# One group of attention scores is issued ahead of the transposes of the next x in TensorE's loop

## What is computed

```
xn = layernorm(x)
q, k = l2norm(xn Wq), l2norm(xn Wk);  v = xn Wv        # 16 heads of 16
p = softmax(q k^T + bias)                              # bias: only 0 <= key - query < 128, minus a slope times the distance
s = (p v) Wo
g = silu(fp4_linear(silu(fp4_linear(xn, w_gate)) * fp4_linear(xn, w_up), w_down))
out = x + s * g
```

## Time and profile before

| | |
|---|---|
| median of 3 runs | 502.65 us (501.77 to 503.2) |
| the profiled execution | 503.14 us, of it a span of 501.4 us in the trace |
| PE busy | 451.2 us, 90% of the span |
| DVE, ACT, POOL busy | 441.2, 402.5, 409.6 us |
| DMA engines, mean over the span | 59 GB/s |

### The profile page before, as it was taken

How to read it: one execution, slowest core, us unless ns; L and a number is a source line. 1 busy time by engine, 2 the same in 40 slices (tenths; PEclk the granted TensorE clock), 3 DMA queues, 4 the chain that set the end, 5 groups by cost and what they waited for, 6 DMA issues and landing times.

```text
span 501.4 us, 14045 instructions
## 1 busy us (share of the span) xinstructions
PE 451.2 (90%) x4990; PEld 314.2 (63%) x4990; DVE 441.2 (88%) x897; ACT 402.5 (80%) x584; POOL 409.6 (82%) x897
## 2 busy tenths in 40 slices
PE   0378889999999999999999999999999999999997
PEld 0144556666667666676767676667666766666665
DVE  4989989999989999989989999988998999887686
ACT  1466988988888888888887888888888888888952
POOL 6544678899988888889997898989999888887751
PEclk9857999999999999999999999999999999999999
DMA  8211011224321314223221222222422121222100
GB/s 300 88 43 44 6 37 44 65 75 76 75 63 45 45 41 67 64 64 64 66 65 43 64 34 54 65 54 54 54 54 54 44 24 43 54 54 54 44 22 33
DMA packets 78276, 29.35 MB, mean 59 GB/s; under 512 B 67712, under 2 KB 77696, under 8 KB 78208
## 3 DMA queue, kind: packets, MB, share of 16 engines
q1 hardware_dynamic: 77920, 28.39, 24.7%
q10 hardware_dynamic: 288, 0.08, 0.1%
HBM read 7.49 MB, written 4.19 MB: 23 GB/s over the span
## 4 chain that ended last, share of the span: by engine, by line
PE 53%; ACT 20%; issue 11%; DVE 10%; POOL 3%; DMA 1%; ACTq 0%; DVEq 0%; POOLq 0%
PE gt L351 10%; PE up L351 10%; PE gt L551 9%; ACT probs L1341 8%; PE bank_q L351 8%; PE bank_b L357 5%; ACT L1341 4%; PE gt L573 4%; ACT pv_t L1219 3%; ACT qk_sq L1319 3%; PE bank_b L598 2%; PE scores L505 2%; PE gt L555 1%; DMA qk_slots<-qk_stack 1%; PE gt L357 1%
## 5 line engine op out<-in xcount | busy, mean ns | idle before, releaser
L1341 ACT ACTIVATE probs<-scores 128x1024 f32<-128x1024 f32 (+1 forms) x101 | 102.2, 1012 | 2.3 <-PE scores L505 1.2
L1526 POOL TENSOR_SCALAR_AFFINE_SELECT probs<-probs 128x512 f32<-128x512 f32 x128 | 81.9, 641 | 1.7 <-ACT probs L1341 1.3
L1533 POOL TENSOR_SCALAR_AFFINE_SELECT probs<-probs 128x512 f32<-128x512 f32 x120 | 76.2, 637 | 3.7
L598 PE MATMUL bank_b<-probs,vals 128*32 128x128 f32 x1952 | 59.7, 274 | 0.6 <-DVE vals L944 0.3
L598 PEld LDWEIGHTS bank_b<-probs,vals 128*32 128x32 f32 x1952 | 51.6, 110 | 7.4 <-issue 5.7
L1219 ACT ACTIVATE qk_stack<-bank_q 128x512 f16<-128x512 f32 x64 | 35.1, 595 | 22.3 <-DVE bank_q L923 22.3
L793 DVE SCALAR_TENSOR_TENSOR xT_lo<-gt,xT_hi 128x512 f16<-128x512 f32 (+1 forms) x34 | 22.3, 657 | 26.3 <-ACT xT_hi L1219 26.3
L551 PE MATMUL gt<-wdn_hi,hT_hi 128*128 128x256 f16 x160 | 43.6, 273 | 0.6 <-DVE hT_lo L845 0.6
L551 PE MATMUL gt<-wdn_hi,hT_lo 128*128 128x256 f16 x160 | 43.6, 273 | 0.0
L551 PE MATMUL gt<-wdn_lo,hT_hi 128*128 128x256 f16 x160 | 43.6, 273 | 0.0
L1563 POOL TENSOR_TENSOR h_q<-h_grid,h_scale 128x704 f32<-128x704 bf16 x31 | 43.1, 1391 | 0.0
(11 more groups left out here) (219 smaller groups left out, 1468.5 us busy)
## 6 DMA issues: line engine op xcount, KB each, us to landing
out<-y SPq DMA_DIRECT2D x32, 128.0 KB, 1.9
x_all<-x SPq DMA_DIRECT2D x20, 128.0 KB, 2.0
x_all<-x SPq DMA_DIRECT2D x3, 512.0 KB, 4.1
x_all<-wproj SPq DMA_DIRECT2D x1, 768.0 KB, 6.9
dn_raw<-wd SPq DMA_DIRECT2D x1, 704.0 KB, 8.7
probs<-wg SPq DMA_DIRECT2D x1, 640.0 KB, 5.3
probs<-wu SPq DMA_DIRECT2D x1, 640.0 KB, 7.6
qk_slots<-qk_stack SPq DMA_TRANSPOSE x32, 3.7
```

The lines of the kernel that those rows point to most:

```text
L598: done = e.matmul(pv_bank(i)[32 * n:32 * n + 32, grp * P:(grp + 1) * P], va, pr, start=part == 0, stop=part == 1 or final(i))
L1341: e.activation(probs[j % P_BUFS][:, grp, :, side(j), :], score_banks(j, grp)[:, :, :, side(j), :].rearrange("p b e h q -> p (b e) h q"), A ...
L1526: e.affine_select(out=own, in_=own, compare_op=ALU.is_ge, fill=0.0, base=0, pattern=[[0, GRP], [-1, P]], channel_multiplier=1).then_inc(s_ ...
L1533: e.affine_select(out=part, in_=part, compare_op=ALU.is_gt, fill=0.0, base=0, pattern=[[0, GRP], [1, P]], channel_multiplier=-1).then_inc( ...
```

## The change

Two lines of TensorE's loop change places. No instruction is added or removed, and every wait stays with its instruction.

```
@@ -666,8 +666,8 @@
             gate_mm_last(2)
             v_mm(4)
             for t in range(4, 31):
+                scores(t - 1, 0)
                 tr_x(t + 1)
-                scores(t - 1, 0)
                 scores(t - 1, 1)
                 pv(t - 3)
                 scores(t - 1, 2)
```

## The result

| | before | changed |
|---|---|---|
| median of 22 runs | 502.18 us | 503.88 us |
| lowest to highest | 501.63 to 503.3 | 502.76 to 505.12 |
| profiled execution, its span | 503.14, 501.4 us | 502.76, 501.0 us |

The account below looks back on a forecast made before the run. A turn was taken as 5.10 us of ScalarE from silu to keep_pv, then about 8.95 us of TensorE. Terms 0 + 0 + 0 + 1.3 us on the 502.65 us median gave 503.9 us; range about 501.9 to 505.8 us.

Parts of the forecast that it names:

- First and second step: TensorE's loop: scores 0 moves into the wait for silu, tr_x unchanged, then scores 1 and pv 0.22 us earlier.
- Third step: Ahead of tr_tail: the 0.22 us only lengthen TensorE's idle time, 0.69 for 0.47 us, behind ScalarE's stretch; 0 us.
- Fourth step: Scores 0's moved wait for the DMA transpose: landings over 1.08 us after silu's start cost the excess; three turns, 1.3 us.
- Rival B: Late transposes weigh more: five to seven turns at 0.5 us, +2.5 to +3.5 us, 505.2 to 506.2 us; chance 0.33.
- the bound of no change: The forecast itself: no change that can be told, between -0.3% and +0.3% (1.5 us); chance 0.59.
- Rival C: TensorE, not ScalarE, holds tr_tail, so 0.22 us is gained each turn: 5.9 us less, 496.7 us; chance 0.08.

Follow-up runs that it names:

- e4: Kernel before (old order) with the four products of scores group 1 repeated three more times, same values, in tiles 3 to 29: 511.13 us, ratio 1.0178.
- e5: Changed kernel (new order) with the four products of scores group 1 repeated three more times, same values: 509.56 us, ratio 1.0152 against the kernel before.
- e1: Kernel before with the two lines swapped only in the 20 loop turns whose DMA transposes had been regular there: ratio 1.0013.
- e2: Kernel before with the two lines swapped only in the seven loop turns whose DMA transposes had been slow there: ratio 1.0021.
- e11: Changed kernel with 64 small float16 products (128 instructions, half a code block) at the head of TensorE's program: 505.13 us, ratio 1.0053 against the kernel before.
- e12: Kernel before (old order) with 64 small float16 products (128 instructions) at the head of TensorE's program: 502.51 us, ratio 0.9999.
- e10: Changed kernel with 64 small float32 products (256 instructions, a whole code block) at the head of TensorE's program: 523.34 us.
- e3: Changed kernel with scores group 0 issued one step further ahead, in front of v_mm of the turn before: 504.67 us, ratio 1.0043 against the kernel before.

## Why the prediction was right, and where it wasn't

First and second step (scores 0 into silu's wait; tr_x no later; pv 0.22 us earlier): as forecast, to 0.01 us, in the timeline after. Turn 17, where a sequence begins, gained 0.03 us (13.36 to 13.33), within the 0.1 us that it was given. With 13.36 us there and 13.81 us in the loop's first turn, the 14.05 us hold for 25 of the 27 turns.

Third step (the gain is hidden by ScalarE, 0 us): right, shown by regular turns of 14.05 us, by idle time of 0.69 us ahead of tr_tail, and by e4 and e5, where taking the cover away makes the 0.22 us appear.

Fourth step (landing minus s+1.08): the mechanism is shown by e1, e2, e11 and e12, and the point was 0.03 us too early: from landing to tr_tail it takes 3.99 us (359.68 to 363.67), not 4.02, since pv to tr_tail takes 2.73 us and not the 2.76 that were read from the loop's first turn. Ten late swapped turns with their excess, from four kernels:

| L | 1.16 | 1.19 | 1.34 | 1.37 | 1.43 | 1.45 | 1.54 | 1.66 | 1.77 | 1.98 |
|---|---|---|---|---|---|---|---|---|---|---|
| excess, us | 0.05 | 0.09 | 0.23 | 0.27 | 0.33 | 0.35 | 0.43 | 0.56 | 0.67 | 0.87 |

Each is L - 1.11 within 0.02 us, and so are four more in e10. Only turn 17, where a sequence begins and the exponentials are half as long, has less slack: in e11 it lost 0.58 us at L = 1.29. The old order's point, by the one turn that passed it (22 of e12), is 1.80, 0.69 us later.

The sum of 1.3 us came out as 1.4 us over the runs, but its three terms didn't hold as turns. I wrote that the same three turns would be late again, by 0.48, 0.53 and 0.33 us. In the profiled execution there were again three, but with turn 20 for 28, and 0.75 us in all; e2 had six and 2.05 us. With the code a whole block further, e10 had four turns and 1.64 us. The number is a draw from a spread, so the agreement of the total to 0.1 us is partly luck, and the range up to six late turns was the honest part. The agreement of 503.88 with 503.9 us is luck as well: the prediction stood on a median of 502.65 us of three runs, where 22 runs gave 502.18, and that made up for a loss that is 1.70 us by the medians. How the spread arises from run to run wasn't measured turn by turn, since each kernel has one trace.

That a packet of the instruction queue beside the transpose goes with its lateness held, with one correction: it must begin in the transfer's first part. By the Trainium skill's page Runtime: NRT & Kernel Launch, section Instruction fetch mechanics, a block is 256 instructions. The counts agree: the queue has 40 packets before, 41 in e10 with 256 instructions more, and 43 in e4 and e5 with 648 more. They don't tell 128 from 256, since e11 and e12 have 41 as well.

Rival B (more than the forecast's three) is what e11 is: the same change with the code 128 instructions further costs 0.53%, outside the bound of no change. Rival C failed by the idle time that it was weighed against, and e4 grew by 8.9 us where it wanted 17.8.

## What to carry to other kernels

Filling an engine's idle time gains only if that time ends on the chain; first look at what the engine waits for next, and whether that moved. When an instruction that waits for a DMA is moved forward, count what then stands behind its wait and compare that with the latest landing of the transfer, not the median: here 0.86 us of margin in regular turns and a loss all the same. A change of no length can still meet other late transfers than the kernel before, so judge a few tenths of a per cent by the turns of the trace and not by totals alone.

## What the hardware showed unexpectedly

A DMA transpose of one tile, in turns 5 to 31 of all 14 traces (378 transposes), took 3.65 to 3.92 us from issue to landing in the 204 cases in which no 16 KB packet of TensorE's code fetch began from 1.5 us before its issue to 4.5 us after. With such a packet begun 0.66 to 2.5 us after the issue it took 4.3 to 6.3 us every time (109 cases); begun 0.14 to 0.35 us after, 3.75 to 4.3 (11 cases); begun before the issue (48), or 3.0 us or later after it (six, five of them in e3), 3.9 us at most. The packet itself takes 1 to 2% of the engines' time in the window. Moving all code by 128 instructions moved the late transposes to other turns, and moving it by 256 brought most of them back.

A float32 product of 128 rows and 16 columns ran as two passes, each with its weight load: 64 of them were 256 instructions, 128 of them products, and took 27.49 us at the program's start, at a granted clock of 1.00; the same 64 in float16 took 1.88 us. The float32 products of pv are doubled too: 32 in the order of rows are 64 in the timeline, so pv is 32 products and not 64. But those 64 take 1.96 us, 0.03 us each, where the 128 took 0.21 us each. What makes the difference was not looked into.
